# Two-batch attention: where SyncE issues the first batch's result stores and the second batch's row loads, against the loads of the seventh group of heads

## What is computed

```python
x = x + 0.5 * ffn(layernorm(x))
x = x + attn(layernorm(x))
x = x + 0.5 * ffn(layernorm(x))

def attn(x):                     # b=2, t=2048, h=16 heads of 16
    q, k, v = rope(split(x @ Wq.T + bq)), rope(split(x @ Wk.T + bk)), split(x @ Wv.T + bv)
    att = softmax(where(tril, q @ k.T / 4, -inf))
    return merge(att @ v) @ Wo.T + bo
```

## Time and profile before

| | |
|---|---|
| timed runs | 1699.5, 1699.5, 1700.61 us; median 1699.5 us |
| profiled execution | 1706.86 us |
| its span (first to last instruction) | 1705.1 us |
| mean granted TensorE clock | 0.962 |
| TensorE matmul busy | 1517.8 us, 89% |
| ScalarE busy | 1014.8 us, 60% |
| VectorE busy | 853.2 us, 50% |
| GpSimd busy | 561.8 us, 33% |
| attention stage | about 640 to 1191 us of the span |

### The profile page before, as it was taken

One profiled execution on the slowest core, in us unless ns is written; L12 is line 12 of the kernel. 1 busy time (PEld: TensorE's weight loads), 2 busy tenths in 40 slices (PEclk: granted clock), 3 DMA queues, 4 the chain that ended last, 5 costly groups with the idle time before them and its releaser, 6 DMA issues. The chain is left out here.

```text
span 1705.1 us, 26544 instructions
## 1 busy us (share of the span) xinstructions
PE 1517.8 (89%) x9943; PEld 1054.2 (62%) x9945; DVE 853.2 (50%) x1844; ACT 1014.8 (60%) x1423; POOL 561.8 (33%) x480
## 2 busy tenths in 40 slices
PE   4999989999975858999999959998499989999996
PEld 3788779898864643333333323333378878888895
DVE  6786467666735740213112122122678656667663
ACT  7323254544515748999999949997732325454541
POOL 3000246656545872111111101110300024665644
PEclk9999999999997988999999979999799999999998
DMA  7221156667534797404314343100722125666653
GB/s 268 69 87 50 52 148 153 150 153 157 130 37 162 215 246 161 67 11 77 58 20 77 57 119 54 24 13 33 263 69 87 50 62 150 150 157 149 151 124 37
DMA packets 120752, 183.14 MB, mean 107 GB/s; under 512 B 19568, under 2 KB 83056, under 8 KB 117360
## 3 DMA queue, kind: packets, MB, share of 16 engines
q1 hardware_dynamic: 91440, 130.04, 29.7%
q0 software_dynamic: 29184, 51.40, 14.5%
HBM read 125.82 MB, written 55.57 MB: 106 GB/s over the span
## 5 line engine op out<-in xcount | busy, mean ns | idle before, releaser
L1720 ACT ACTIVATE 8048_pr<-8048_pS 128x1024 f32<-128x1024 f32 x448 | 421.4, 1079 | 36.0 <-PE 8048_pS L1641 34.8
L1671 PE MATMUL 8048_pO<-8048_pr,6230_vres 128*32 128x512 f32 x1792 | 239.3, 606 | 4.4 <-DVE 8048_tO L1745 3.6
L1641 PEld LDWEIGHTS 8048_pS<-sq_rows,sk_rows 50*128 50x128 f32 x896 | 74.7, 186 | 214.7 <-ACT 8048_pr L1720 156.8
L1641 PE MATMUL 8048_pS<-sq_rows,sk_rows 50*128 50x512 f32 x896 | 185.7, 467 | 24.3 <-DMA sq_rows<-shift 19.8
L1745 DVE STREAM_TRANSPOSE 8048_tO<-8048_pO 128x512 f32<-128x512 f32 (+1 forms) x33 | 23.0, 698 | 310.1 <-PE 8048_pO L1671 310.1
L170 PE MATMUL 91_pGU<-columns_XT,weights_wts 128*128 128x512 f32 x384 | 153.6, 400 | 7.0 <-DVE columns_XT L853 4.6
L170 PE MATMUL 14723_pGU<-columns_XT,weights_wts 128*128 128x512 f32 x384 | 153.6, 400 | 7.0 <-DVE columns_XT L853 4.5
L1734 POOL TENSOR_SCALAR_AFFINE_SELECT 8048_pr<-8048_pr 128x512 f32<-128x512 f32 x32 | 21.4, 669 | 400.2 <-ACT 8048_pr L1720 400.2
L171 PE MATMUL 91_pGU<-columns_XT,weights_wts 128*128 128x512 f32 x384 | 151.1, 393 | 0.0
L171 PE MATMUL 14723_pGU<-columns_XT,weights_wts 128*128 128x512 f32 x384 | 150.8, 393 | 0.0
L172 PE MATMUL 14723_pGU<-columns_XT,weights_wts 128*128 128x512 f32 x384 | 150.7, 392 | 0.0
(11 more groups left out here) (315 smaller groups left out, 3423.3 us busy)
## 6 DMA issues: line engine op xcount, KB each, us to landing
token_table<-weights_xn POOLq DMA_DIRECT2D x16, 512.0 KB, 6.2
91_raw_g<-WgT SPq DMA_DIRECT2D x16, 512.0 KB
91_raw_u<-WuT SPq DMA_DIRECT2D x16, 512.0 KB
91_raw_d<-WdT SPq DMA_DIRECT2D x16, 512.0 KB
q_rows<-rows_half SPq DMA_DIRECT2D x32, 256.0 KB, 3.4
k_rows<-rows_half SPq DMA_DIRECT2D x32, 256.0 KB, 3.6
sq_rows<-q_rows SPq DMA_DIRECT2D x32, 256.0 KB
sk_rows<-k_rows SPq DMA_DIRECT2D x32, 256.0 KB
```

Of the source, the lines that this page charges most:

```text
L1641: m = t_.matmul(to[:, e, :], key, query, start=True, stop=True)
L1671: m = t_.matmul(pO[e * 32:(e + 1) * 32, off:off + wd], vres[:, (g // GB) * TPB + kt, at:at + 32], from_(e), start=n == first[j], stop=n == ...
L1720: s_exp.done(a.activation(to, pS[:, u % RING, :, :], ACT.Exp, scale=HD ** -0.5))
```

## The change

In SyncE's program the block that belongs to g = 6 is moved from behind the transfers of g = 6 to in front of the wait that stands before them. Nothing is added or taken away, and no other engine's program changes.

```diff
                 for g in range(2, NG):
+                    if g == 6:
+                        for m in range(4):
+                            store(m)
+                        for m in range(4):
+                            sp.wait_ge(*s_out[m].at(1))
+                            residual(4 + m)
                     over = max(u for u, (kind, a_, b_) in enumerate(units)
                                if (kind == "pair" and blocks[whole[a_ // 2][0]][0] == g - 2) or (kind == "cut" and blocks[a_][0] == g - 2))
                     sp.wait_ge(*s_S.at(over + 1))
                     for hh in range(GH):
                         self.load_head(sp, g, hh)
                         self.load_shift(sp, g, hh)
-                    if g == 6:
-                        for m in range(4):
-                            store(m)
-                        for m in range(4):
-                            sp.wait_ge(*s_out[m].at(1))
-                            residual(4 + m)
                 for m in range(4, 8):
                     store(m)
```

## The result

The changed kernel took 1680.63 us (median of 4 runs, 1679.68 to 1685.31) against 1700.05 us for the one before (4 runs, 1699.5 to 1704.12). The ratio of the two is 0.9886, with a 95% interval of 0.9862 to 0.991. That is 19.4 us less. The forecast was 20.8 us less, to 1678.7 us, in a range of 1675.5 to 1685.0.

A forecast was written before the change was run, and what follows sets the result against it. The prediction took ScalarE to set the pace, with some 21 us lost in the sixth group's stretch to late rows of x. The removed stall of 20.8 us gave 1699.5 - 20.8 = 1678.7 us, range 1675.5 to 1685.0.

The forecast's parts named there:

- The bottleneck: Sixth group's stretch: late rows of x hold VectorE's with_bias(4), then TensorE's projection piece, then ScalarE; some 21 us lost.
- ScalarE sets the pace: Second, fourth and fifth groups: ScalarE busy 62.5 to 63.5 us of 64.09 to 65.62 us, TensorE close behind.
- Steps 1 to 3: SyncE's queue: stores go from 909.73 us, block 4's rows arrive before 976.11, g = 6's transfers still start at 965.38.
- The cover of 42 us: g = 6's transfers: loads begun as late as 1007 us instead of 965.38 would do, so added waits cost nothing.
- Step 4: g = 5's transfers, sharing DMA engines with stores 0 and 1: no delay that costs time; kept as a rival, 0.02.
- its 36 us: g = 5's transfers: two stores at worst 18.2 us each, so at the outside g = 5 lands 36 us later, at 961.
- Step 5: Sixth group's stall: 1.86 us of ScalarE's 22.58 us wait stays, so 20.72 us goes; by whole stretches 20.80 us.
- the twin: Second group: same planner steps as the sixth, its rows loaded long before; stretch 65.62 us, ScalarE waits 1.86 us.
- The level: Whole kernel: 20.8 us off the timed median of 1699.5 us gives 1678.7 us.
- profiled excess of 7.36 us: Profiled execution over timed median: if all lay in this queue's transfers, the timed stall would be 13.4 us; partial-gain rival 0.09.
- The clock: Sixth group's stretch, clock 0.88: nothing added to the gain; rival of 10.4 us more, 1668.3 us, chance 0.01.
- at most some 1.2 us: Sixth group's stretch: TensorE busy 63.80 us against 62.63, so at most this much of matmuls ran longer.

The follow-up runs named there:

- e1: Against the kernel before: the moved block stands behind the wait for group 4's scores but in front of g = 6's transfers; 1689.57 us, ratio 0.9871.
- e2: Against the changed kernel: only the four stores stay in front, row loads go back behind g = 6's transfers; 1704.67 us, ratio 0.9965 to the kernel before.
- e3: Against the changed kernel: only store 0 and the row load of block 4 stay in front; 1686.27 us, ratio 0.9841 to the kernel before.
- hold_380: Against the changed kernel: g = 6's transfers held until unit 380; 1680.14 us, against 1680.54 for the changed kernel in the same series.
- hold_404: Against the changed kernel: g = 6's transfers held until unit 404 of 408; 1709.48 us, ratio 0.9995 to the kernel before.
- front_of_g5: Against the changed kernel: the moved block one group further forward, in front of g = 5's wait and transfers; 1698.53 us, ratio 0.9968 to the kernel before.
- after: The changed kernel in its first measurement, against the kernel before; 1680.63 us, ratio 0.9886; the profiled execution took 1681.33 us.
- after_again: The changed kernel itself, run again in the second series; 1680.54 us, ratio 0.9856 to the kernel before.

## Why the prediction was right

1. **The bottleneck** was read from three views that agree: a stretch 21 us too long with ScalarE's usual work in it, a chain VectorE, TensorE, ScalarE of waits of 20.11, 21.32 and 22.58 us, and the queue's order. Experiments e1 to e3 show it: the stall goes when the rows of block 4 alone come ahead of the heads, and stays at 16 us when only the stores do. "ScalarE sets the pace" is too strong: in the fifth group TensorE was as busy (63.58 against 63.45 us of 64.09), and e1 shows that ScalarE waits as soon as TensorE's work gets longer.
2. **Steps 1 to 3, when the transfers go**: stores from 909.7 expected, 908.74 measured; row loads at 947.3 against 946.48; `residual(7)` between 950 and 965, issued by 949.7; g = 6 at 965.4 against 964.56. The cover of 42 us holds: 39 us later costs nothing (hold_380), and hold_404, which costs all, gives some 41 us as an estimate.
3. **Step 4, group 5**: no wait for its heads showed in the profile after, with stores 0 and 1 behind them. The step took the landing times of stores that queue behind the heads as delays of the heads; its 36 us was a far bound. front_of_g5 shows what a real delay would have been.
4. **Step 5, the twin**: 20.72 and 20.80 us were predicted; 22.58 - 1.86 = 20.72 us and 86.42 - 65.05 = 21.37 us came. One slip in the text: the twin's piece stands in step 78 and the sixth group's in 350, which is 272 units or four groups on, and not 136. The choice of the twin doesn't hang on it.
5. **The level**: 1680.63 against 1678.7. That the profiled excess of 7.36 us over the median might lie in the stall did not come true: the gain of the medians is 19.4 and 22.8 us. The feed-forwards alone differ by 5 us each from one execution to another. That the absolute time came out within 2 us is in part luck: the kernel before has medians from 1700.05 to 1710.52 us in its four sets of runs, a spread wider than the range forecast. What the prediction carries is the gain.
6. **The clock**: by the rule of the Trainium skill, "TensorE: Matmul & The Clock Gate", section Terms, the gain would have been 31.2 us and the time 1668.3. Measured were 19.4 to 22.8 us and 1680.63, so the measurement speaks against adding it to a wait. The time at the lower level was nearly all time in which TensorE had nothing to run. The step's "at most some 1.2 us" is 1.6 us against the sixth group's own stretch after the change, and it holds for that stall only. A short wait can cost more in clock than in waiting, as e1 shows (1.9 us more of ScalarE's wait at the first piece, 5.1 us more of stretch); the twin was taken from an execution in which the clock held, and in four of nine it is 3 us longer.

## What to carry to other kernels

A queue that waits in program order should have its transfers in the order in which their first reader is due, and a wait in it is free only in a gap in which nothing behind it is due. Look for the gap on both sides, since one group further forward gave back 18 of 23 us. Price a stall by a twin of the same stretch that doesn't have it, and look at several executions of the twin. Ask of a late transfer how many steps lie between the waiting instruction and the next thing that the bottleneck engine needs from behind it. With 3 steps (block 4) a wait of 0.84 us reached TensorE whole, with 19 steps (block 5) one of 1.69 us didn't.

## What was not expected of the hardware

After the same TensorE wait of 1.56 us, with the same instructions behind it, the granted clock fell in four of nine profiled executions and held in five. Where it fell, TensorE's busy time for the 499 matmuls of the second group went from 62.6 to 65.6 us and the group from 65.6 to 68.6 us. At the first piece of block 4, behind a wait of 1.58 us, it fell in one of six (hold_404) and held in five (after, after_again, e3, hold_380, front_of_g5). After waits of 0.6 us or less at these pieces it held each time, and from 775 to 835 and from 840 to 895 us, in the third and fourth group, it was 1.00 in all thirteen executions. That the wait brings it about is likely by these counts, and not shown. Why the same wait falls on one side or the other was not tried.

The Trainium skill, "TensorE: Matmul & The Clock Gate", section "Wait — 56ns, not 53.3ns?", gives the time from one 512-column matmul to the next as about twice as long at the lower level. The rows here agree roughly for whole runs of instructions: the eight value matmuls of front_of_g5 take 1.93 us against 1.06, a factor of 1.8. The 1.86 us in e1 end just where the clock comes back.
